# Inverse image transforms by halves with the first half's norm between them, and the second half's norm and routing moved into the first expert block, in a four-layer block network

## What is computed

```python
x = x + _L1_conv_ref(_ln_c(x), ...)      # per-image 7x7 depthwise filters
t = t + _L1_ffn_ref(_ln_t(t), ...)       # 8 experts, the best 2 of each token count

# _L1_conv_ref
key = softmax(einsum('bchw,oc->bohw', x, K_w) + K_b)             # 49 keys per image
filters = einsum('bcn,bnk->bck', query, key)
filters = conv0(filters); filters = relu(norm(filters) * ln_w + ln_b)
filters = einsum('bcij,oc->boij', filters, conv1_w) + conv1_b
out = depthwise_conv(x, filters, padding=3)

# _L1_ffn_ref
top_logits, top_idx = top_k(x @ Wg, 2); top_w = softmax(top_logits)
out = sum over e of combine[:, e] * (silu(xt @ W1[e]) @ W2[e])   # 128 -> 512 -> 128
```

## Time and profile before

| | us |
|---|---|
| median of 3 runs | 411.04 |
| lowest, highest | 409.38, 413.88 |
| the profiled execution, whole time | 410.04 |
| its span, first to last instruction | 408.3 |
| TensorE busy in it | 386.3 |
| ScalarE, VectorE, Pool busy | 282.5, 258.3, 152.6 |

### The profile page before, as it was taken

How to read it: one execution, slowest core, us unless ns; L and a number is a source line. 1 busy time by engine, 2 the same in 40 slices (tenths; PEclk the granted TensorE clock), 3 DMA queues, 4 the chain that set the end, 5 groups by cost and what they waited for, 6 DMA issues and landing times.

```text
span 408.3 us, 5044 instructions
## 1 busy us (share of the span) xinstructions
PE 386.3 (95%) x1641; PEld 273.7 (67%) x1641; DVE 258.3 (63%) x557; ACT 282.5 (69%) x502; POOL 152.6 (37%) x126
## 2 busy tenths in 40 slices
PE   8999989989999889999999999999999999988993
PEld 3588656443646667787787767877777777655782
DVE  0654246884342688566774995766957497777774
ACT  4241235945210967777979989999999998887881
POOL 3810000740085427421458584121232366332253
PEclk9999999999999999999999999999999999999998
DMA  8940000000000023571111004034040002120331
GB/s 263 451 165 0 2 1 0 1 2 0 0 2 0 1 64 109 219 284 53 26 32 46 0 8 125 28 80 177 3 129 26 27 26 79 52 79 0 104 101 56
DMA packets 10674, 28.77 MB, mean 70 GB/s; under 512 B 1079, under 2 KB 2231, under 8 KB 10392
## 3 DMA queue, kind: packets, MB, share of 16 engines
q1 hardware_dynamic: 10648, 28.45, 20.5%
HBM read 27.82 MB, written 0.62 MB: 70 GB/s over the span
## 4 chain that ended last, share of the span: by engine, by line
PE 64%; ACT 17%; DVE 15%; issue 3%; POOLq 0%; POOL 0%; ACTq 0%; DVEq 0%
PE ps L411 16%; PE ps L412 15%; PE ps L413 15%; ACT hidh L966 5%; ACT ps L967 4%; PE ps L418 3%; DVE hidl L1287 2%; PE ps L656 2%; PE ps L423 2%; ACT rstd L875 2%; ACT rstd L877 2%; PE ps L602 1%; DVE bot L1209 1%; DVE small L1208 1%; PE ps L646 1%
## 5 line engine op out<-in xcount | busy, mean ns | idle before, releaser
L1287 DVE TENSOR_TENSOR hidl<-ps,hidh 128x512 fp32r<-128x512 f32 x160 | 108.6, 687 | 52.7 <-ACT ps L967 51.1
L382 POOL TENSOR_TENSOR x<-x,parts 128x512 f32<-128x512 f32 x43 | 55.8, 1298 | 148.1 <-DVE parts L1297 99.7
L411 PE MATMUL ps<-xh,wh_all 128*128 128x512 f32 x160 | 73.0, 456 | 2.2 <-DVE hidl L1287 1.3
L966 ACT ACTIVATE hidh<-ps,par 128x512 fp32r<-128x512 f32 x96 | 68.1, 709 | 8.5 <-PE ps L413 6.8
L411 PE MATMUL ps<-hidh,wh_all 128*128 128x512 f32 (+1 forms) x162 | 64.3, 397 | 4.4 <-DVE hidl L1287 3.8
L967 ACT ACTIVATE ps<-ps,par 128x512 f32<-128x512 f32 x96 | 65.4, 681 | 0.0
L412 PE MATMUL ps<-hidh,wl_all 128*128 128x512 f32 (+1 forms) x162 | 63.5, 392 | 0.0
L412 PE MATMUL ps<-xh,wl_all 128*128 128x512 f32 x160 | 63.5, 397 | 0.0
L413 PE MATMUL ps<-hidl,wh_all 128*128 128x512 f32 (+1 forms) x162 | 63.3, 390 | 0.0
L413 PE MATMUL ps<-xl,wh_all 128*128 128x512 f32 x160 | 63.0, 393 | 0.0
L372 POOL TENSOR_TENSOR wl_all<-wa,wh_all 128x512 fp32r<-128x512 f32 x40 | 50.7, 1283 | 3.5
(11 more groups left out here) (227 smaller groups left out, 569.2 us busy)
## 6 DMA issues: line engine op xcount, KB each, us to landing
scores_all<-rows_scratch SPq DMA_DIRECT2D x48, 256.0 KB, 3.3
wa<-in_moe SPq DMA_DIRECT2D x2, 4096.0 KB, 16.5
wa<-in_moe SPq DMA_DIRECT2D x1, 2048.0 KB, 9.4
dft_x<-in_dft_x SPq DMA_DIRECT2D x1, 640.0 KB
dft_o<-in_dft_o SPq DMA_DIRECT2D x1, 640.0 KB
w<-in_w_bottom SPq DMA_DIRECT2D x1, 576.0 KB, 7.0
w<-in_w_out SPq DMA_DIRECT2D x1, 576.0 KB, 8.8
cst<-in_consts SPq DMA_DIRECT2D x1, 512.5 KB, 7.8
```

The lines of the kernel that those rows point to most:

```text
L382: pool.tensor_tensor(half(x, h), half(x, h), parts[:, n % 2, :], ALU.add).then_inc(s["state_added"], 1)
L411: pe.matmul(o, wh, xhi, start=start, stop=False)
L966: act.activation(hidh[:, n % 2, f, :], sums, func, bias=bias).then_inc(s["hidden_hi_act"], 1)
L1287: dve.tensor_tensor(hidl[:, n % 2, f, :], bank(sums_bank(n, f)), f32(hidh[:, n % 2, f, :]), ALU.subtract).then_inc(s["hidden_lo"], 1)
```

## The change

1. **Filters twice.** The ReLU's result is written twice into `filt_two`, 113 columns wide, at columns 0 and 64, the 15 between being zero, so that the conv1 matmul puts `filt_t` on partitions 0 to 48 and 64 to 112. The table `dft_k` is loaded to both places. Even frequency blocks use the lower copy, odd ones the upper. Four transforms are issued in a row into banks 5, 6, 7 and 4.
2. **Inverse by halves.** Images 0 and 1 go through all five blocks, then images 2 and 3. Centre and variance of half 0 stand in the second round, before blocks 2 and 4. VectorE computes xn of half 0 ahead of adding images 2 and 3 to x.
3. **Block 0.** Norm, logits and routing of half 1 go to the places that they have in blocks 1 and 2. turn_route(0) comes between the third and fourth quarter of step 0; in front(0) a wait for the second half's addition stands before the third quarter, whose bank images 2 and 3 used.
4. **Pool** splits experts 4 and 5 after `img_back` 2, and 0 to 3 after both ReLUs. Norm 3 uses banks 6 and 7 in both halves. keep_clock is four matmuls instead of five.

```diff
-            sp.dma_start(dft_k[:], dram["dft_k"]).then_inc(s["dft_loaded"], 16)
+            for first in (0, KEYS - KK):
+                sp.dma_start(dft_k[first:first + KK, :], dram["dft_k"]).then_inc(s["dft_loaded"], 16)
...
-            pool.wait_ge(s["filt_act"], 1)
+            pool.wait_ge(s["filt_act"], 2)
...
-            pool.wait_ge(s["norm_lo"], 6)
+            pool.wait_ge(s["img_back"], 2)
...
-                last = pe.matmul(bank(4, KK, C, b * C), filt[:, 3, b, :], p("conv1_w"), start=True, stop=True)
+                last = pe.matmul(bank(4, KEYS, C, b * C), filt_two[:, b, :], p("conv1_w"), start=True, stop=True)
...
-                pe.matmul(bank(fring[q % 3]), dft_k[:, q * C:(q + 1) * C], filt_t[:], start=True, stop=True).then_inc(s["filt_freq"], 1)
...
+                rows = slice(0, KK) if q % 2 == 0 else slice(KEYS - KK, KEYS)
+                pe.matmul(bank(fring[q % 4]), dft_k[rows, q * C:(q + 1) * C], filt_t[rows, :], start=True, stop=True).then_inc(s["filt_freq"], 1)
+
+            for q in range(4):
+                filt_freq(q)
             pe.wait_ge(s["img_freq_kept"], QF)
-            for q in range(QF):
-                if q + 2 < QF:
-                    filt_freq(q + 2)
-                pe.wait_ge(s["freq_mult"], q + 1)
-                for b in range(B):
-                    last = pe.matmul(bank(b, cols=PIX), prod_f[:, q, b * C:(b + 1) * C], dft_o[:, q, :],
-                                     start=(q == 0), stop=(q == QF - 1))
-                    if q == QF - 1 and b % 2:
-                        last.then_inc(s["img_back"], 1)
+            for h in range(2):
+                for q in range(QF):
+                    if h == 0 and q == 1:
+                        filt_freq(4)
+                    if h == 1 and q == 2:
+                        center(3, 0)
+                    elif h == 1 and q == 4:
+                        variance(3, 0)
+                    if h == 0:
+                        pe.wait_ge(s["freq_mult"], q + 1)
+                    for b in (2 * h, 2 * h + 1):
+                        last = pe.matmul(bank(b, cols=PIX), prod_f[:, q, b * C:(b + 1) * C], dft_o[:, q, :],
+                                         start=(q == 0), stop=(q == QF - 1))
+                last.then_inc(s["img_back"], 1)
...
-            norm(3)
-            keep_clock(5, 0)
+            keep_clock(4, 0)
             logits(0)
-            front(0)
-            logits(1)
-
-            for n in range(E):
-                first_half(n)
-                if n == 0:
+            for f in range(4):
+                if f == 2:
+                    pe.wait_ge(s["x3_ready"], 2)
+                front(0, (f,))
+
+            for j in range(E):
+                first_half(j)
+                if j == 4:
+                    variance(3, 1)
+                elif j == 5:
+                    logits(1)
+                elif j == 7:
+                    turn_route(1)
+                if j == 0:
+                    front(1, (2,))
+                    back(0, (2,))
                     turn_route(0)
-                second_half(n)
-                if n == 3:
-                    turn_route(1)
+                    front(1, (3,))
+                    back(0, (3,))
+                else:
+                    second_half(j)
+                if j == 3:
+                    pe.wait_ge(s["rows_ready"], 1)
+                    center(3, 1)
...
-            norm(3)
-            for h in range(2):
-                high_part(3, h)
+            square(3, 0)
+            inverse_root(3, 0)
+            high_part(3, 0)
...
+                    elif (n, f) == (4, 3):
+                        square(3, 1)
+                    elif (n, f) == (5, 1):
+                        act.preload_act_table_set("natural_log_exp_and_others")
+                        inverse_root(3, 1)
+                        act.preload_act_table_set("silu_and_others")
+                    elif (n, f) == (5, 2):
+                        high_part(3, 1)
...
+            step(dve.memset(filt_two[:, :, KK:KEYS - KK], 0.0))
...
-            dve.tensor_scalar(flat(f3), flat(f1), 0.0, None, ALU.max).then_inc(s["filt_act"], 1)
+            for first in (0, KEYS - KK):
+                last = dve.tensor_scalar(filt_two[:, :, first:first + KK], f1, 0.0, None, ALU.max)
+                last.then_inc(s["filt_act"], 1)
...
+                if h:
+                    norm_half(3, 0)
                 dve.wait_ge(s["img_back"], h + 1)
```

More of the change, by code:

```diff
@@ L34 @@
 KK = KW * KW
+KEYS = 64 + KK
 POOL_T = 5
@@ L232, in center_bank @@
         def center_bank(n, h):
[L233 removed]
+            return h if n < 3 else 6
         def variance_bank(n, h):
[L236 removed]
+            return 2 + h if n < 3 else 7
         def work(t, n, h):
@@ L1006, in _ @@
                     hidden(n, f)
-                    if n < 2 and f == 1:
-                        route_tanh(n)
+                    if (n, f) == (0, 0):
+                        route_tanh(0)
+                    elif (n, f) == (4, 3):
[6 more added lines that the diff above has]
+                        high_part(3, 1)
+                    elif (n, f) == (6, 1):
+                        route_tanh(1)
             for kb in (1, 2):
@@ L1251, in _ @@
             dve.wait_ge(s["filt_done"], 1)
-            f0, f1, f2, f3 = [filt[:, j] for j in range(4)]
+            f0, f1, f2 = [filt[:, j] for j in range(3)]
             def flat(t):
@@ L1463, in _ @@
             route_shares(0)
-            for f in range(4):
-                low(1, f)
-                if f == 0:
-                    route_start(1)
-                elif f == 1:
-                    keep_rows(0)
-            route_pick(1)
-            for f in range(4):
-                if f == 3:
-                    scale(0)
-                    scale(1)
-                low(2, f)
-                if f == 1:
-                    route_exps(1)
-                elif f == 2:
-                    route_two(1)
-            route_shares(1)
-            for n in range(3, E + 1):
+            for n in range(1, E + 1):
                 for f in range(4):
-                    if f == 3:
+                    if f == 3 and n == 2:
+                        scale(0)
+                        scale(1)
+                    elif f == 3 and n > 2:
                         scale(n - 1)
                     low(n, f)
-                if n == 5:
-                    keep_rows(1)
+                    if (n, f) == (1, 0):
+                        keep_rows(0)
+                    elif (n, f) == (5, 1):
+                        norm_half(3, 1)
+                    elif (n, f) == (5, 2):
+                        norm_low(3, 1, 6)
+                    elif (n, f) == (5, 3):
+                        route_start(1)
+                    elif (n, f) == (6, 0):
+                        route_pick(1)
+                    elif (n, f) == (6, 2):
+                        route_exps(1)
+                    elif (n, f) == (7, 0):
+                        route_two(1)
+                    elif (n, f) == (7, 1):
+                        route_shares(1)
+                    elif (n, f) == (8, 1):
+                        keep_rows(1)
             for kb in (1, 2):
```

36 lines of the change are left out of this document (16 added, 20 removed).

## The result

The changed kernel takes 408.99 us in the median of 20 runs (406.76 to 412.70), the kernel before 411.76 us (409.32 to 414.68, 20 runs): ratio 0.9931, interval 0.9905 to 0.9957. The profiled execution took 406.97 us with a span of 405.0 us, where the one before had 410.04 and 408.3. So the change gains 2.8 us in the median and 3.1 us between the two profiled executions; 3.0 had been forecast. The interval leaves out 1, so the gain is clear of the noise, and it is smaller than 1%, the case that the forecast gave 0.65 to.

A forecast was written before the change was run, and what follows sets the result against it. TensorE was taken as the bound, busy 386.3 of the 408.3 us span. Step 1 5.6 us earlier, less 2.5 and 0.1, gave 3.0: 407.0 from 410.04 or 408.0 from the median; stated 407.5, range 404.8 to 411.5.

The forecast's parts named there:

- Filter copies, +0.3: Before the transforms: running the ReLU twice adds 0.3 us, bounds 0.2 and 0.5, so transforms start at 116.67.
- Four transforms in 1.85 us: Filter transforms: pairs on different row strips overlap fully, four taking 2 x 0.92 = 1.85 us; saving bounded by 0 and 1.85.
- Rival 1: Filter transforms: the row pairs run one after another, costing 1.85 us, for 409.4 us; chance 0.15.
- Inverse and norm of half 0: Stage before block 0: inverse ends at 130.40 with centre and variance inside; experts could start at 133.29.
- xl 0.4 us longer: VectorE before the first expert: Pool's splits hold up xl, adding 0.4 us, so experts start at 133.7.
- 0.5 us of waiting for the routing: First expert to step 1: of the 1.54 us wait for turned routing weights, 0.5 is left, bounds 0 and 1.0.
- 2.53 us back in the block: Block 0 on TensorE: half 1's centre and variance (0.86 each) and logits (0.81) cost 2.53 us there.
- rival 5: Better than forecast: no lock on xl, no routing wait, no backlog, perhaps a 0.29 us gap gone; 406.2 us, chance 0.19.
- Routing rows of half 1, no cost: Block 0: rows stored about 183.5, first used 8.7 us later in step 9, the weight load over; no cost.
- Rival 4: Step 9 of block 0: half 1's routing rows come late, a wait of 0.7 or 1.4 us, 408.9 us; chance 0.05.
- Rival 2: xl and routing operations wait a whole Pool instruction twice, 2.56 us instead of 0.4, for 409.7 us; chance 0.12.
- Rival 3: Block 0: ScalarE's 5.1 us of norm work come out on TensorE's path, for 412.6 us; chance 0.06.

The follow-up runs named there:

- One strip: The changed kernel with all transforms on partitions 0 to 48; end 283.80 us after the first filter transform, against 282.09 for the changed kernel.
- Norm behind: The changed kernel with centre and variance of half 0 after the whole inverse; end 284.76 us after the first filter transform, against 282.09.
- Pool after routing: The changed kernel with Pool splitting experts 4 and 5 only after half 0's routing; end 280.95 us after the first filter transform, against 282.09.
- four more loads: The changed kernel with four extra table loads (5.12 us) on ScalarE in block 0; end 288.88 us after the first filter transform, against 282.09.
- pairs alone: The kernel before with only doubled filters and table and four transforms in a row; end 283.62 us after the first filter transform, against 285.55.
- two more loads: The changed kernel with two extra table loads (2.56 us) on ScalarE in block 0; end 285.06 us after the first filter transform, against 282.09.
- no keep_clock: The changed kernel without the four matmuls on zeros ahead of half 0's logits; end 285.45 us after the first filter transform, against 282.09.
- Centre in the wait: The changed kernel with half 1's centre matmul moved ahead of half 0's logits, replacing two keep_clock matmuls; end 281.17 us after the first filter transform, against 282.09.

## Why the prediction was right

The case that was given the largest chance came, near its middle: 3.1 us between the profiled executions against 3.0. By its steps:

- *Filter copies, +0.3.* The ReLU pair takes 0.43 against 0.26 us, the conv matmuls start 0.23 later, and the transforms 0.09 later (116.46 for a forecast 116.67), as the image transforms between are 0.1 us shorter.
- *Four transforms in 1.85 us.* 2.00. "One strip" shows that nothing but the strips does it. My 0.92 per transform was misread: the 2.77 us of three hold about 0.2 us that a group pays once. Four in a row on one strip take 3.63, so a fourth costs 0.86, and the saving is 1.63, not 1.85. Rival 1 (0.15, "Row pairs run one after another") is out. The rows on the score stage were the right evidence, though of another shape.
- *Inverse and norm of half 0.* Forecast end 130.40, measured 130.13. Counted from the first transform: 13.73 against 13.67. In part small errors cancel: the transforms took 0.15 more, centre and variance 0.85 and 0.86 instead of 0.92 and 0.91. "Norm behind" confirms that centre and variance inside buy 1.89 us at the expert.
- *xl 0.4 us longer.* It was 0.43 us longer, and "Pool after routing" gave 0.44 back.
- *0.5 us of waiting for the routing.* The size held, the place was wrong. The turned weights are not waited for at all: VectorE has the shares ready 9.54 us behind the start of the logits (10.06 before), and TensorE wants them 9.72 us behind it (8.58 before). Instead the copy L1373, held by Pool, delays a hidl (wait 0.29). First expert to step 1 is 9.69 us for a forecast 9.6, and 9.15 without Pool beside it, about the 9.10 that I had got with no wait.
- *Step 1 at 143.3.* 143.16: 5.7 us earlier for 5.6.
- *2.53 us back in the block.* 2.25 to block 1's centre. That is 2.53 less the 0.29 us gap of the kernel before, which went; I had kept that gap apart, in rival 5.
- *ScalarE's backlog, 0.1 of bounds 0 and 0.9.* Nothing.
- *Routing rows of half 1, no cost.* SP's own rows (the store's issue and the issues of the broadcasts behind it):

```profile
184.24 0.28 SPq L288 DMA_DIRECT2D rows_scratch<-rows  x1
...
185.72 1.75 SPq L297 DMA_DIRECT2D scores_all<-rows_scratch  x4
```

The first broadcast is issued 1.5 us behind the store, where it was 6.1 us beside the weight load (issued at 160.81 here, 23 us ahead of the store), and no wait for scores follows. Rival 4 is out.

The rest of the rivals. Rival 2 (0.12, "Pool and VectorE exclude each other all along the path") was half right: three operations met Pool, two of them on TensorE's path, and together they cost 0.98 us at step 1, between my 0.4 and its 2.56. My step "Pool is through with experts 4 and 5 by 138, before most of the routing" failed: the part of the routing that lies before 138 was enough. I had also looked at operations with two inputs only; the costly one was a copy of 128x8 from SBUF to SBUF. That its cost didn't show as an error in the sum is luck: it took the room that I had given to the routing's own chain.

Rival 3 (0.06, the 5.1 us of norm work come out on TensorE) was not borne out, and the runs show by how little. It "decides where ScalarE's slack per step doesn't absorb it", the text said. What there was is 0.86 us: with 2.56 us more on ScalarE TensorE waits 1.71. Its price might have been too low as well: the 4.25 us wait of "four more loads" moved the end by 6.79.

Rival 5 got one thing right, the 0.29 us gap; the rest of it, the lock, was there to be had only by "Pool after routing".

Still open: how far the 0.76 us of clock in "norm behind" belongs to its longer waits, since each variant's trace is one execution; and how the 1.53 us that separates "pairs alone" from the change splits between the halves, the second half's norm and Pool's order, since no run has the halves alone.

## What to carry to other kernels

When work is moved from a stage with gaps into a full one, price what the full one takes back first (here 2.25 of 5.8 us), and look for pieces that still fit in the gaps: the centre and Pool's order, found in the same rows, were worth another 1.85 us. A wait that is taken away may have kept another engine quiet; count every operation that it now meets, the small ones too, with what is queued behind them. And measure a small change from a mark just ahead of it, not from the span.

## What the runs showed that I hadn't expected

*A wait can cost more than its length.* In four variants the granted clock of TensorE fell from 1.00 to 0.50 (2.4 to 1.2 GHz) in or behind waits that the changed kernel doesn't have: 1.71 us (two more loads), 4.25 (four), 1.30 and 0.76 with the logits between (no keep_clock), and 0.69, 1.30 and 0.89 (norm behind). It was low for 3.4 us in the first and the last of these and for 6.8 in the other two, with expert matmuls 0.43 us apart for 0.23, and it cost 0.8 to 1.8 us each time. With 18 matmuls on zeros in the 4.25 us wait it stayed at 1.00.

But a wait of such a length doesn't always bring it. The kernel before stood still for 1.54 us ahead of the turned weights, and its clock was 1.00 around it. And far behind the change every profiled execution has this wait, here in the kernel before:

```profile
361.78 0.50 PE L411 MATMUL ps<-hidh,wh_all 128*128 128x512 f32 x1 [1.61 <-DVE hidl L1287]
```

It is 1.60 to 1.63 us long in all 14, and the clock stayed at 1.00 in 13 of them; only in "no keep_clock" did it fall there, from 361.0 on. So a wait can have a second price, in the worst case here as large as the wait, and what decides whether it falls due, these runs don't say.

*The clock also falls without a new wait.* "Pairs alone" had the same waits in front of its experts as the kernel before (0.23 and 0.82), and its clock was 0.85 over the 11.47 us behind, where the kernel before had 1.00. "Centre in the wait" had this 9 us ahead of its first filter transform, with TensorE busy from 105 to 115 us:

```profile
108.00:110.00 2.00, 2.00 (x4) 0.97 (x4) 0.36 (x2) 0.00 (x0) 0.00 (x0) 0.50 0.00 0
```

The low clock lasted from 105.0 to 111.9 there, which is why its T is late, and such stretches are why one execution's span says little about an edit of 1 us.

*Two strips side by side.* The Trainium skill (TensorEngine Tiling, Key Properties) has tiles run in parallel; here two strips of 49 rows in fp32, two passes each, ran four transforms in 1.99 us for 3.70 on one strip. Of the drain at a change of tiling mode that it speaks of, no run here gives the cost by itself. What rows show is that a centre matmul on all 128 partitions, between inverse matmuls, costs 0.85 us from start to start (125.83 to 126.68), and a transform on 49 partitions with the same 128x512 output 1.05 (119.49 to 120.54), while one more transform in a row costs 0.86. So a group of transforms pays some 0.2 us once, 0.28 in the row of pairs (2.00 less twice 0.86), and a drain, if it is that, is in these.
